# Attention softmax by bias on ScalarE, and expert weights split in two parts with waits of their own

## What is computed

```
logits = einsum("bqhd,bkhd->bhqk", rope(ln(x) @ Wq), rope(k)) * 0.25      # 32 heads of 16
w      = softmax(logits)                                                   # over 128 keys
x      = x + tanh(g_xattn) * ((w @ v) @ Wout + bout)
probs  = softmax(ln(x) @ gate_w.T); weights, selected = top_k(probs, 6)    # 16 experts
moe    = sum over selected of weight * (silu(xf @ gate_e) * (xf @ up_e)) @ w2_e   # inner width 352
shared = the same with one shared expert of inner width 704
x      = x + tanh(g_ffn) * (moe + shared)
```

## Time and profile before

| | |
|---|---|
| median of 3 runs | 1808.34 us (1804.49 to 1809.41) |
| the profiled execution's own time | 1808.88 us |
| its span, first to last instruction | 1807.0 us |
| PE busy | 1625.6 us, 90% |
| PE weight loads | 1340.6 us, 74% |
| DVE, ACT, POOL busy | 738.4, 499.3, 670.7 us |
| mean granted TensorE clock | 0.885 |

### The profile page before, as it was taken

One profiled execution on the slowest core, in us unless ns is written; L12 is line 12 of the kernel. 1 busy time (PEld: TensorE's weight loads), 2 busy tenths in 40 slices (PEclk: granted clock), 3 DMA queues, 4 the chain that ended last, 5 costly groups with the idle time before them and its releaser, 6 DMA issues.

```text
span 1807.0 us, 32322 instructions
## 1 busy us (share of the span) xinstructions
PE 1625.6 (90%) x9026; PEld 1340.6 (74%) x9027; DVE 738.4 (41%) x1527; ACT 499.3 (28%) x986; POOL 670.7 (37%) x1135
## 2 busy tenths in 40 slices
PE   4999999999999992299999999999999999879998
PEld 2666666666666652188888888888888888869997
DVE  3556565565555554022222222222222222234555
ACT  3334333333333330022222222222222222211111
POOL 2224333333334336322633333333333330164342
PEclk8788777787877755599999999999999999989999
DMA  4002211111112214423333333333333332245563
GB/s 159 16 27 75 106 71 62 62 62 62 62 62 90 74 60 156 157 71 125 119 119 124 125 119 119 125 125 119 119 121 123 124 119 72 87 143 189 160 194 119
DMA packets 76310, 190.53 MB, mean 105 GB/s; under 512 B 10497, under 2 KB 12546, under 8 KB 73570
## 3 DMA queue, kind: packets, MB, share of 16 engines
q1 hardware_dynamic: 54562, 99.81, 17.3%
q0 software_dynamic: 21696, 90.06, 13.7%
HBM read 117.07 MB, written 72.76 MB: 105 GB/s over the span
## 4 chain that ended last, share of the span: by engine, by line
PE 46%; POOL 7%; DVE 3%; issue 2%; SPq 1%; ACT 0%; DMA 0%; DVEq 0%; POOLq 0%
PE bank L1306 27%; PE bank L1334 14%; POOL w_lo L219 3%; PE bank L1285 2%; PE bank L1315 2%; POOL w_lo L212 2%; POOL w_hi L208 2%; DVE tree L1394 1%; POOL w_hi L205 1%; DVE comb L1399 0%; DVE tree L1396 0%; SPq L1137 0%; DVE tree L1397 0%; DVE x_lo L1368 0%; SPq L1138 0%
## 5 line engine op out<-in xcount | busy, mean ns | idle before, releaser
L1306 PE MATMUL bank<-w_hi,x_hi 128*128 (+1 forms) x1152 | 294.1, 336 | 44.0 <-issue 25.3
L1306 PE MATMUL bank<-w_lo,x_hi 128*128 (+1 forms) x1152 | 279.8, 324 | 0.0
L1306 PE MATMUL bank<-w_hi,x_lo 128*128 (+1 forms) x1152 | 279.6, 324 | 0.0
L1306 PEld LDWEIGHTS bank<-w_hi,x_hi 128*128 128x128 f32 x1152 | 194.8, 189 | 70.4 <-issue 70.4
L205 POOL CAST w_hi<-w_raw 128x512 fp32r<-128x512 f32 (+1 forms) x54 | 31.0, 612 | 534.6 <-PE bank L1334 534.6
L1385 DVE SCALAR_TENSOR_TENSOR act<-silu,row_w,bank 128x352 f32<-128x352 f32 x112 | 65.0, 581 | 386.6 <-issue 199.5
L1257 ACT ACTIVATE silu<-bank 128x352 f32<-128x352 f32 x144 | 66.9, 464 | 530.2 <-PE bank L1306 530.2
L1306 PEld LDWEIGHTS bank<-w_lo,x_hi 128*128 128x128 f32 x1152 | 202.1, 189 | 0.0
L1306 PEld LDWEIGHTS bank<-w_hi,x_lo 128*128 128x128 f32 x1152 | 201.8, 189 | 0.0
L630 PE MATMUL bank<-k_t,q_t 32*128 32x256 f32 x512 | 197.6, 519 | 1.4 <-ACT k_t L579 1.4
L1334 PE MATMUL bank<-w_hi,a_hi 128*128 (+3 forms) x432 | 172.7, 400 | 2.2 <-DVE a_lo L1374 1.6
(11 more groups left out here) (184 smaller groups left out, 2612.8 us busy)
## 6 DMA issues: line engine op xcount, KB each, us to landing
xr<-expert_rows SPq DMA_DIRECT2D x112, 264.0 KB, 2.7
y_rows<-y SPq DMA_DIRECT2D x112, 256.0 KB, 2.0
w_raw<-in_w POOLq DMA_DIRECT2D x18, 1408.0 KB, 6.7
w_raw<-in_w POOLq DMA_DIRECT2D x18, 512.0 KB, 7.6
x_sb<-in_x SPq DMA_DIRECT2D x16, 256.0 KB, 3.0
x_res<-in_x SPq DMA_DIRECT2D x16, 256.0 KB, 4.1
x_rows<-x SPq DMA_DIRECT2D x16, 256.0 KB, 4.4
x_rows<-row SPq DMA_DIRECT2D x16, 256.0 KB, 4.5
```

What stands on the lines that cost most here:

```text
L1306: last = nc.tensor.matmul(to[:, 0:WIDTH], xx[jt][:, d, :], w[d][half][:, cols], start=(d == 0 and xx is x_hi and w is w1_hi), stop=(d == D ...
```

## The change

The exponential takes the maximum as a bias. DVE only scales it: `smax` times -SCALE, four numbers per row. ACT makes four exponentials of one head each, straight from PSUM.

The weights are split by two functions with a semaphore each (`w1_made`, 8 per expert, and `w2_made`, 3 per expert). Experts 0 and 1 are split in rounds 1, 2, 4 and 5 of phase_a; in phase_b the w1 part waits for the last `up` of expert e-2 and the w2 part for its last `down`. `down` now waits for `w2_made`, for which it reads the expert again, and the two values that `up` needs are read ahead of `down`.

The transposes of `k_cos` move from slot 5 to slot 6 on PE; ACT copies `q_t` at the start of slot 5 and `k_t` at the start of slot 7, ahead of that slot's exponential.

```diff
+        def split_w1(pool, e):
+            pool.wait_ge(w1_in, 16 * (e + 1))
...
+            for d in range(DC):
+                pool.wait_ge(w_hi_made, 11 * e + 2 * d + 2)
+                for half in range(2):
+                    nc.gpsimd.tensor_tensor(w1_lo[d][half][:, s], w1_raw[:, d, halves[half]],
+                                            w1_hi[d][half][:, s].bitcast(F32), ALU.subtract).then_inc(w1_made, 1)
+        def load_after_split(pool, e):
+            pool.wait_ge(w1_made, 8 * e)
+            pool.wait_ge(w2_made, 3 * e)
+            load_w(nc.gpsimd, e)
 # POOL, phase_a
+            def early_weights(r):
+                if r in (1, 4):
+                    split_w1(pool, r // 3)
+                if r in (2, 5):
+                    split_w2(pool, r // 3)
+                    load_after_split(pool, r // 3 + 1)
-                    if isinstance(at(PLACE)[0], int) and at(PLACE)[0] == BATCHES - 3:
-                        split_w(pool, 0)
-                        pool.wait_ge(w_made, 8)
-                        load_w(nc.gpsimd, 1)
-                    if isinstance(at(PLACE)[0], int) and at(PLACE)[0] == BATCHES - 1:
-                        split_w(pool, 1)
+                if at(LOAD) and isinstance(at(LOAD)[0], int):
+                    early_weights(at(LOAD)[0])
 # ACT, attend
-                    a.activation(soft[u % 2][:], soft[u % 2][:], ACT.Exp, scale=SCALE).then_inc(exp_done, 1)
+                    need(act, prob_mm, b * GROUPS + u - 1)
+                    for h in range(4):
+                        last = a.activation(soft[u % 2][:, h, :], bank[2 + u % 2][:, h * P:(h + 1) * P], ACT.Exp,
+                                            bias=smax[u % 2][:, h:h + 1], scale=SCALE)
+                    last.then_inc(exp_done, 1)
 # PE, scores and project
-                    need(pe, shifted, b * GROUPS + u - 1)
+                    need(pe, exp_done, b * GROUPS + u - 1)
-                if u == 5:
+                if u == 6:
                     pe.wait_ge(k_rope_done, b + 1)
                     pe.wait_ge(qt_done, b + 1)
                     four_transposes(bank[0], k_rope).then_inc(kt_mm, 1)
 # DVE, attend
+                need(dve, exp_done, b * GROUPS + u - 1)
                 v.tensor_reduce(smax[u % 2][:], s3, AX.X, ALU.max).then_inc(smax_done, 1)
                 dve.wait_ge(smax_done, b * GROUPS + u + 1)
-                need(dve, prob_mm, b * GROUPS + u - 1)
-                v.tensor_tensor(soft[u % 2][:], s3, smax[u % 2][:, :, None].to_broadcast([P, 4, P]), ALU.subtract)\
-                    .then_inc(shifted, 1)
+                v.tensor_scalar(smax[u % 2][:], smax[u % 2][:], -SCALE, None, ALU.mult).then_inc(shifted, 1)
 # POOL, phase_b
-                pool.wait_ge(w_made, 8 * e)
-                load_w(nc.gpsimd, e)
+                waits_apart(pool, passed_pool, (h_mm, last))
+                split_w1(pool, e)
                 waits_apart(pool, passed_pool, (y_mm, last))
-                split_w(pool, e)
+                split_w2(pool, e)
+                if e + 1 < EXPERTS + SHARED:
+                    load_after_split(pool, e + 1)
 # PE, down
                     off = pe.value_load(table[0:1, bass.ds(g * T_N + T_W2, 1)], min_val=0, max_val=D)
+                    e = pe.value_load(table[0:1, bass.ds(g * T_N + T_EXPERT, 1)], min_val=0, max_val=EXPERTS - 1)
+                    ready = 3 * (e + 1)
...
+                w1_block = w1_at(i, at)
                 pe.wait_ge(a_lo_done, g + 1)
+                pe.wait_ge(w2_made, ready)
```

More of the change, by code:

```diff
@@ L196, in load_w @@
             eng.dma_start(w2_raw[0:96, 2, :], w2[e, 2, 0:96]).then_inc(w2_in, 16)
-        def split_w(pool, e):
-            s = e % SLOTS
+        def split_w1(pool, e):
+            s = slice(e % SLOTS * WIDTH, (e % SLOTS + 1) * WIDTH)
+            halves = [slice(0, WIDTH), slice(WIDTH, 2 * WIDTH)]
             pool.wait_ge(w1_in, 16 * (e + 1))
+            for d in range(DC):
+                for half in range(2):
+                    nc.gpsimd.tensor_copy(w1_hi[d][half][:, s], w1_raw[:, d, halves[half]]).then_inc(w_hi_made, 1)
+            for d in range(DC):
+                pool.wait_ge(w_hi_made, 11 * e + 2 * d + 2)
+                for half in range(2):
+                    nc.gpsimd.tensor_tensor(w1_lo[d][half][:, s], w1_raw[:, d, halves[half]],
+                                            w1_hi[d][half][:, s].bitcast(F32), ALU.subtract).then_inc(w1_made, 1)
@@ L203, in split_w, with split_w2 @@
+        def split_w2(pool, e):
+            s = slice(e % SLOTS * D, (e % SLOTS + 1) * D)
             pool.wait_ge(w2_in, 32 * (e + 1))
             for c, (_, m) in enumerate(WC):
[L205 to L209, removed]
+                nc.gpsimd.tensor_copy(w2_hi[c][0:m, s], w2_raw[0:m, c, :]).then_inc(w_hi_made, 1)
@@ L210, in split_w @@
             pool.wait_ge(w_hi_made, 11 * (e + 1))
             for c, (_, m) in enumerate(WC):
[L212 to L222, removed]
+                nc.gpsimd.tensor_tensor(w2_lo[c][0:m, s], w2_raw[0:m, c, :], w2_hi[c][0:m, s].bitcast(F32),
+                                        ALU.subtract).then_inc(w2_made, 1)
@@ L542, in one_round @@
                             .then_inc(at_hi_done, 1)
+                    if at(PROJECT) and u == 5:
+                        b, j, n = at(PROJECT)
+                        act.wait_ge(qt_mm, b + 1)
+                        need(act, score_mm, (b - 1) * GROUPS)
+                        a.activation(q_t[j][:].rearrange("p c n -> p (c n)"), bank[0][:], ACT.Copy)\
+                            .then_inc(qt_done, 1)
+                    if at(PROJECT) and u == 7:
+                        b, j, n = at(PROJECT)
+                        act.wait_ge(kt_mm, b + 1)
+                        need(act, score_mm, (b - 1) * GROUPS)
+                        k4 = bank[0][:].rearrange("p (c n) -> p c n", c=DC)
+                        a.activation(k_t[j][:, :, 0, :], k4, ACT.Copy, scale=const[:, C_EVEN:C_EVEN + 1])\
+                            .then_inc(kt_done, 1)
+                        a.activation(k_t[j][:, :, 1, :], k4, ACT.Copy, scale=const[:, C_ODD:C_ODD + 1])\
+                            .then_inc(kt_done, 1)
                     attend(at, u)
@@ L1052, in phase_b @@
 def phase_b(nc, sb, sem, bank, const, ident, table, table_in, ends_i, pad_at, pads_out, slots_all, y_step, tanh2,
-            scattered, load_w, split_w, w1_hi, w1_lo, w2_hi, w2_lo, w_made, h_mm, y_mm,
+            scattered, split_w1, split_w2, load_after_split, w1_hi, w1_lo, w2_hi, w2_lo, w1_made, w2_made, h_mm, y_mm,
             rows, y_rows, x1_rows, x2_rows, out):
@@ L1337, in down @@
                 last.then_inc(y_mm, 1)
+                return w1_block
             pe.wait_ge(table_in, 16)
@@ L1343, in one_step @@
                     transpose_x(0, 0, 0)
-                if live(i, -2):
-                    down(i, at)
+                w1_block = down(i, at) if live(i, -2) else w1_at(i, at)
                 if starts_tile(i, 1):
@@ L1350, in one_step @@
                 if live(i, 0):
-                    up(i, at)
+                    up(i, at, *w1_block)
             steps(pe, one_step)
```

44 lines of the change are left out of this document (16 added, 28 removed).

## The result

The changed kernel takes **1867.5 us** (median of 4, 1861.2 to 1871.4), against 1808.2 before: a ratio of 1.033, 95% interval 1.029 to 1.036. The forecast was slower, 1827 us with a range of 1790 to 1855. The sign was right, and the time lies 12 us above the range.

What follows compares the result with a forecast made beforehand. PE was taken to bound the kernel, its granted clock setting the pace. Terms +43 + 8 + 0 − 16 − 7 + 2 − 12 = +18 on 1808.9 gave 1827 us, range 1790 to 1855.

Steps and rivals of the forecast that it cites:

- The loads ahead of `down`: Phase_b loop: value loads before `down` delay it, steps of 7.39 and 7.89 us against 7.23, +43 us in 104 steps.
- The lead of 17 matmuls: Phase_b: PE's sequencer runs at most 17 matmuls ahead, so `up` is fully issued only 1.0 us after it starts.
- No load is before `up`, the rest is as in the shared steps: Phase_b: from `down` to the next `up` takes 2.79 us, as in shared steps, since nothing loads before `up`.
- The rival that the loads are hidden: Phase_b: PE's queue takes all of `up`, loads run under it; +6 instead of +43, 1790 us; chance 0.15.
- `k_cos` behind `row`: Phase_a: transposes of `k_cos` moved after `row` leave 0.88 us still to do, clock uncertain; +8 us (−20 to +20).
- (b): Round of batch 13: without expert 0's split there, DVE's 6.96 us operation and PE's 7.65 us wait go; −7 us.
- (c): Rounds 1, 2, 4 and 5: early split may delay DVE's row operations, but paired subtractions let DVE in; +2 (0 to +8).
- Rival C: Phase_a loses: `k_cos` stretches the slow part, or DVE's tiny multiplication waits behind POOL's subtractions; +25, 1850 us; chance 0.15.
- Softmax: Attention groups: DVE saves about 0.5 us, ACT's four exponentials take 1.3 and lose about 0.7, covered by PE; 0 us.
- The weights: Splitting expert weights early, three pieces in phase_a and at its end; −21 us in all.
- (a): End of phase_a: without expert 1's split all engines meet about 16 us earlier, the drain stays; −16 us.
- The end: Last split in phase_b: w1's part starts about 9.5 us earlier, PE's 15.40 us wait shrinks; −12 us (−9.5 to −15).

## Why the prediction was wrong

**The loads ahead of `down`: right mechanism, +43 forecast, +53.6 measured.** The lead of 17 matmuls held: it put the sequencer at the loads 1.0 + 0.1 us after `up` begins, and the trace has 1.05. In the mean `down` came at 4.69 and 5.05 us (4.6 and 5.1 forecast). What was short is the rest of the step: 2.89 us from `down` to `up`, not 2.79, since after the idle time 0.34 us pass between the starts of `down`'s first two matmuls (1313.77 and 1314.11), against 0.23 between the next. That makes steps of 7.58 and 7.93, a mean 0.12 above 7.64, in 104 steps 12 us. "No load is before `up`, the rest is as in the shared steps" was the step that was off. The rival that the loads are hidden fell. Its own price was a little low: by its terms (0.7 + 0.1 + 3.1 + 0.4, then 2.79) the steps are 7.09 and 7.59, not 7.04 and 7.54, and the term is +11, not +6.

**`k_cos` behind `row`: +8 (−20 to +20) forecast, +39 alone.** This is the step that failed and made the prediction wrong. The chain to `row` came as forecast (8.08 against 7.97 us), and the wait for `q_t` was worth nothing. By the estimate T − H/2 the work cost 2 us, not even the 11. What was mis-sized is the clock. The prediction had the granted clock fall about here in each round and left open whether it comes back earlier or later, for at most 20 us either way, and took +8 for work and clock together. The fall stayed where it was, but the clock then stays low for 27 us in place of 17 and 24 by turns, 33 us in 13 rounds. The bound of 20 us had no row behind it. In the changed kernel itself the move has no run of its own: phase_a's +24.0, with the 7.65 us won back (b) and some 5 lost (c), leaves an estimated +27 for it. Rival C had the right direction, and it had 0.15. Why the clock stays low longer is open.

**Softmax: 0 forecast, 0.9994 of before measured.** ACT's stage took 1.14 us, where I took 1.3. The Trainium skill ("ScalarE: Activation LUTs", What ACT_TABLE_LOAD costs) gives an estimated 1.27 us by its figures; the measured 1.14 is nearer to it than to either of my bounds.

**The weights, −21 forecast.** (a) The change of phases gave 21.8 instead of 16, but the first steps lost 5.5 again, 16.3 together. In the first steps PE's wait for the transfer of `xr` is 8.83 us, 4.05 before; why it grew is not shown. (b) and (c) were forecast as −7 and +2. The 7.65 us wait went, as forecast. For (c) I argued that subtractions in pairs with waits let DVE in. They do not: the two POOL rows join without a gap (145.86 + 3.44, then 149.28), and `xn` took 10.50 us, where it takes 0.55 in other rounds. Against the run with the move alone that round is 5 us longer (46.2 and 41.2). The early split moved this collision and did not remove it.

**The end, −12 forecast, −8.9 measured.** −13.7 at the split as worked out, and 4.63 us of it back through the late gathers, of which I had allowed 2.4.

In sum, phase_a went 24 us up instead of 3, and the loop 54 instead of 43; the other stretches came to −25 instead of −28.

## What to carry to other kernels

A register load in front of a block of matmuls is not free because work is queued: here PE's sequencer is ahead by only 17 matmuls, and 0.76 us for each load must fit into what these take. Put the reads right behind the matmuls of the stage before, ahead of the next wait; that gave 52 us to a kernel whose PE was 96% busy in the loop (726.4 of 753.1 us). Where the granted clock changes within a round, moving 0.9 us of PE work out of a gap can cost more than 0.9 us, so read how long the low stretch lasts, not only where it begins; and test with work that nothing uses.

## What the runs showed of the hardware

Adding matmuls whose result nothing uses made the kernel faster in every place tried around `row`: 28 a round took H from 256 to 99 us and the time from 0.958 to 0.932 of before. By the estimate T − H/2 the work rose meanwhile from 411 to 439 us, and T fell from 539.0 to 488.2. The kernel has rounds of the same instructions with different lengths (40.9 and 44.4 us), and can stay in one kind for ten rounds in a row.

The lead of PE's sequencer was the same in the changed kernel: in the step shown above it had issued `up` 1.05 us after `up` began (1310.15 and 1309.09), with 7 of the 24 matmuls begun. The Trainium skill ("TensorE: Matmul & The Clock Gate", Architectural detail: the array is 16× 32×32) gives a queue of 64; the steps with three and four loads do not agree with it, if matmuls and weight loads are what it counts.

One DVE operation that takes 0.55 us in other rounds ran for 10.50 us, from 146.17 to 156.67, beside 16 casts and subtractions of POOL, and ended within 0.3 us of the last of them. The kernel before has one of 6.96 us beside the split in the round of batch 13, and the kernel with the new split and neither softmax part nor move has one of 7.82 beside its own.
